# First attention of a four-layer megakernel: sums of two or four window offsets before the output product

## The reference, cut to what matters

```python
        q = _pointwise(Wq, bq, x)
        k = _pointwise(Wk, bk, cond)
        v = _pointwise(Wv, bv, cond)
        k = jnp.pad(k, ((0, 0), (0, 0), (pad_left, pad_right)))
        v = jnp.pad(v, ((0, 0), (0, 0), (pad_left, pad_right)))
...
        dots = jnp.einsum('bhdt,bhdtw->bhtw', qh, k_win) * scale
        attn = jax.nn.softmax(dots, axis=-1)
        out = jnp.einsum('bhtw,bhdtw->bhdt', attn, v_win)
        out = out.reshape(B, C, T)
        return _pointwise(Wo, bo, out)
```

## Time and profile before

| | |
|---|---|
| median of 3 runs | 1675.38 us (1674.85 to 1675.93) |
| the profiled execution's own time | 1682.93 us |
| its span | 1681.6 us |
| mean granted TensorE clock over the span | 0.981 |
| first wide product starts | 119.73 us into the span |
| last addition of `attn0` ends | 238.4 us |
| wide products and what hangs on them | 118.7 us, 7% of the span |

### The profile page before, as it was taken

One profiled execution on the slowest core, in us unless ns is written; L12 is line 12 of the kernel. 1 busy time (PEld: TensorE's weight loads), 2 busy tenths in 40 slices (PEclk: granted clock), 3 DMA queues, 4 the chain that ended last, 5 costly groups with the idle time before them and its releaser, 6 DMA issues.

```text
span 1681.6 us, 22246 instructions
## 1 busy us (share of the span) xinstructions
PE 1602.4 (95%) x9380; PEld 1156.9 (69%) x9380; DVE 1003.3 (60%) x1328; ACT 470.8 (28%) x682; POOL 567.4 (34%) x402
## 2 busy tenths in 40 slices
PE   8979989999989999999999999998999999899998
PEld 2264437888658877788787878877755466568786
DVE  5987765223552665564555646554762379786765
ACT  4140012000422334233432323332101456531010
POOL 3907642221244334131432313231132054462211
PEclk9989979999989999999999999999999999999999
DMA  3000032100200211011010110100210121500000
GB/s 127 1 1 0 1 123 79 50 0 32 100 13 0 85 41 63 20 44 38 26 38 26 63 38 26 38 1 1 104 49 1 26 53 28 193 1 13 13 13 13
DMA packets 18019, 66.55 MB, mean 40 GB/s; under 512 B 1440, under 2 KB 9760, under 8 KB 13312
## 3 DMA queue, kind: packets, MB, share of 16 engines
q1 hardware_dynamic: 17920, 65.12, 11.2%
HBM read 58.82 MB, written 2.10 MB: 36 GB/s over the span
## 4 chain that ended last, share of the span: by engine, by line
PE 80%; DVE 12%; ACT 3%; issue 2%; POOL 2%; DMA 1%; SPq 0%; DVEq 0%; ACTq 0%; POOLq 0%
PE banks L270 47%; PE banks L264 27%; PE banks L399 2%; DVE arena L442 2%; PE banks L1913 1%; DVE arena L1434 1%; DVE grouped_split L1466 1%; PE banks L2186 1%; PE banks L1320 1%; DVE arena L234 1%; DVE arena L1421 1%; DVE window L483 1%; ACT arena L1537 1%; ACT arena L1536 1%; POOL up_lo L859 1%
## 5 line engine op out<-in xcount | busy, mean ns | idle before, releaser
L270 PE MATMUL banks<-grouped_split 128*128 128x512 f32 x1536 | 367.4, 395 | 6.8 <-DVE grouped_split L1466 6.1
L270 PEld LDWEIGHTS banks<-grouped_split 128*128 128x128 f32 x1536 | 284.7, 189 | 70.0 <-DVE grouped_split L1466 9.3
L1603 POOL TENSOR_TENSOR arena<-arena,attn_tables 128x512 f32<-128x512 f32 x80 | 102.1, 1281 | 312.7 <-ACT arena L1537 312.7
L270 PE MATMUL banks<-experts_split 128*128 128x512 f32 (+1 forms) x792 | 181.6, 392 | 1.9 <-DVE experts_split L630 1.9
L270 PEld LDWEIGHTS banks<-experts_split 128*128 128x128 f32 (+1 forms) x792 | 146.5, 185 | 36.4 <-issue 2.5
L1421 DVE TENSOR_TENSOR arena<-banks,attn_tables 128x512 f32<-128x512 f32 x80 | 54.7, 684 | 129.9 <-ACT arena L1537 129.9
L264 PE MATMUL banks<-arena 128*128 128x64 f32 (+2 forms) x698 | 111.9, 313 | 14.7 <-DVE arena L1434 6.8
L264 PEld LDWEIGHTS banks<-arena 128*128 128x128 f32 x698 | 96.5, 196 | 36.3 <-issue 27.7
L660 DVE SCALAR_TENSOR_TENSOR arena<-banks,experts,arena 128x512 f32<-128x512 f32 x64 | 47.6, 750 | 106.8 <-PE banks L270 106.8
L1434 DVE TENSOR_TENSOR arena<-arena 128x512 f32<-128x512 f32 x80 | 70.5, 881 | 54.6 <-POOL arena L1603 54.5
L509 POOL TENSOR_TENSOR window<-window 128x1024 f32<-128x1024 f32 x32 | 75.7, 2368 | 73.9 <-DVE window L483 73.9
(11 more groups left out here) (289 smaller groups left out, 2961.3 us busy)
## 6 DMA issues: line engine op xcount, KB each, us to landing
grouped<-in_attn SPq DMA_DIRECT2D x16, 1024.0 KB, 5.0
experts<-in_expert SPq DMA_DIRECT2D x8, 1024.0 KB, 4.8
linear<-in_ffn SPq DMA_DIRECT2D x1, 4096.0 KB, 13.3
grouped<-in_attn SPq DMA_DIRECT2D x8, 512.0 KB, 3.6
dense<-arena SPq DMA_DIRECT2D x16, 256.0 KB, 4.3
dense<-in_w SPq DMA_DIRECT2D x1, 3584.0 KB, 12.0
dense<-in_attn SPq DMA_DIRECT2D x1, 3072.0 KB, 13.5
dense<-in_w SPq DMA_DIRECT2D x1, 2688.0 KB, 10.2
```

What stands on the lines that cost most here:

```text
L270: s = pe.matmul(dst, lhsT=lhsT[i], rhs=rhs[j], start=(k == 0 and x == 0), stop=(k == n - 1 and x == 2))
L1603: g_.tensor_tensor(rot, rot, SIN[:, h * HALF:(h + 1) * HALF], ALU.mult).then_inc(rot_sin.sem, 1)
```

## The change

It changes five things in `attn0`.

1. **Sums.** The 16 offsets of a pair of tiles are dealt into groups of 4, 2, 2, 4, 2, 2. A group of two has one sum, a group of four has three (0+1, 2+3, and the sum of these). GpSimd does 40 sums in place of 32; TensorE does 24 x 2 output matmuls in place of 32 x 2.
2. **Places.** Wide products have three places in PSUM (`WIDE`) in place of two; the accumulators of the output have one pair of banks in place of two. There are 12 slots in place of 8; four of them lie in the memory of k.
3. **Order.** An output product is due 6 offsets behind the last of its group (group of four, or the first group) or 4 behind it, and its two matmuls stand at two neighbouring offsets.
4. **Low parts.** They are computed by four offsets over all 512 positions instead of by 128 positions over all offsets. The first is computed before the first wide product; the other three follow the products n = 0, 3 and 7 on VectorE. ScalarE's last cut of the high part is written in four pieces.
5. **Fillers.** `stay_busy` issues 13 matmuls in place of 22; the additions of a pair of tiles stand at offset 5, its moments at 7 and 9.

```diff
+    SLOTS, SUM = [K0 + j * 2 * D for j in range(4)] + [DOTS + j * 2 * D for j in range(8)], PROD + 2048
+    sizes = (4, 2, 2, 4, 2, 2)
+    groups = [(p * WIN + sum(sizes[:i]), n) for p in range(4) for i, n in enumerate(sizes)]
+    sums = [(first, pair) for first, size in groups for pair in (((0, 1), (2, 3), (0, 2)) if size == 4 else ((0, 1),))]
...
+    WIDE = (0, 2, 6)
...
-        stay_busy(m, pe, 7, 22)
+        stay_busy(m, pe, 7, 13)
...
-        pe.wait_ge(*low_done(4))
...
+        def to_out(k, x):
+            first, size = groups[k]
+            p, i = k // len(sizes), k % len(sizes)
+            pe.wait_ge(*pair_done(last_sum[first] + 1))
+            if i == 0 and p:
+                pe.wait_ge(*add_done(2 * p))
+            s = mm(pe, bank[:, 4 + x, :], f(W0 + 3 * P, P), f(SLOTS[first % 12] + x * D, D), i, len(sizes))
+            if x:
+                s.then_inc(out_mm.sem, 1)
+
+        due = [first + size - 1 + (6 if size == 4 or first % WIN == 0 else 4) for first, size in groups]
         for n in range(4 * WIN):
             p, w = n // WIN, n % WIN
-            if n >= 2:
-                pe.wait_ge(*av_done(n - 1))
+            if n >= 3:
+                pe.wait_ge(*av_done(n - 2))
+            if n % 4 == 0 and p == 0:
+                pe.wait_ge(*low_done(w // 4 + 1))
             for x, part in enumerate((hi, lo)):
                 for i, t in enumerate(PAIRS[p]):
                     rows = slice(t // 2 * 32, t // 2 * 32 + 32)
-                    s = pe.matmul(bank[:, n % 2 * 2 + i, :], lhsT=seltr[rows, t * P:(t + 1) * P], rhs=part[rows, w, :],
+                    s = pe.matmul(bank[:, WIDE[n % 3] + i, :], lhsT=seltr[rows, t * P:(t + 1) * P], rhs=part[rows, w, :],
                                   start=x == 0, stop=x == 1)
             s.then_inc(wide_mm.sem, 1)
-            if n % 2 and n >= 5:
-                to_out((n - 5) // 2)
-        to_out(30)
-        to_out(31)
+            for k in range(len(groups)):
+                for x in range(2):
+                    if due[k] + x == n:
+                        to_out(k, x)
...
-        divide(0)
-        for c in range(1, 4):
+        for c in range(4):
             divide(c)
-            low(c - 1)
-        low(3)
+        low(0)
...
             v.wait_ge(*wide_mm(n + 1))
-            if n >= SLOTS:
-                v.wait_ge(*out_mm((n - SLOTS) // 2 + 1))
...
+            if n - 12 in summed:
+                v.wait_ge(*pair_done(summed[n - 12] + 1))
+            elif n >= 12:
+                v.wait_ge(*out_mm([first for first, size in groups].index(n - 12) + 1))
...
+            if n in (0, 3, 7):
+                low({0: 1, 3: 2, 7: 3}[n])
+            if n in (3, 5, 7, 9):
+                v.wait_ge(*low_done((n - 1) // 2))
-            if w == 7 and p:
+            if w == 5 and p:
                 add(p - 1)
+            if w in (7, 9) and p:
+                moments(p - 1, (w - 7) // 2)
...
+        for n, (first, (to_step, other_step)) in enumerate(sums):
+            to, other = (f(SLOTS[(first + x) % 12], 2 * D) for x in (to_step, other_step))
+            if (to_step, other_step) == (0, 2):
+                g.wait_ge(*pair_done(n))
+            else:
+                g.wait_ge(*av_done(first + other_step + 1))
+            g.tensor_tensor(to, to, other, ALU.add).then_inc(pair_done.sem, 1)
...
-            act.activation(hi[:, :, cut], dots[:, :, cut], ACT.Copy).then_inc(hi_done.sem, 1)
+            for ws in [slice(0, WIN)] if c < 3 else [slice(4 * j, 4 * j + 4) for j in range(4)]:
+                act.activation(hi[:, ws, cut], dots[:, ws, cut], ACT.Copy).then_inc(hi_done.sem, 1)
```

More of the change, by code:

```diff
@@ L299, in attn0 @@
     ATT = DOTS + WIN * D
-    AV, SLOTS, SUM = DOTS, 8, PROD + 2048
+    SLOTS, SUM = [K0 + j * 2 * D for j in range(4)] + [DOTS + j * 2 * D for j in range(8)], PROD + 2048
+    sizes = (4, 2, 2, 4, 2, 2)
+    groups = [(p * WIN + sum(sizes[:i]), n) for p in range(4) for i, n in enumerate(sizes)]
+    sums = [(first, pair) for first, size in groups for pair in (((0, 1), (2, 3), (0, 2)) if size == 4 else ((0, 1),))]
+    summed = {first + pair[1]: n for n, (first, pair) in enumerate(sums)}
+    last_sum = {first: n for n, (first, pair) in enumerate(sums)}
     seltr = m.buf("selt_split", CT, NT * P, F32R)
@@ L307, in attn0 @@
     sub_done, exp_done, sum_mm, sum_done, att_done, hi_done, low_done = (
-        m.sem(n, 4) for n in ("sub", "exp0", "sum_mm", "sum_done", "att", "att_hi", "att_low"))
+        m.sem(n, k) for n, k in (("sub", 4), ("exp0", 4), ("sum_mm", 4), ("sum_done", 4), ("att", 4), ("att_hi", 7), ("att_low", 4)))
     selt_done, wide_mm, av_done, pair_done, out_mm = (
-        m.sem(n, k) for n, k in (("selt_done", 1), ("wide_mm", 64), ("av_done", 64), ("pair_done", 32), ("out0_mm", 32)))
+        m.sem(n, k) for n, k in (("selt_done", 1), ("wide_mm", 64), ("av_done", 64), ("pair_done", len(sums)), ("out0_mm", len(groups))))
     add_done = m.sem("add0_done", NT)
@@ L398, in tensor @@
                     rows = slice(t // 2 * 32, t // 2 * 32 + 32)
-                    s = pe.matmul(bank[:, n % 2 * 2 + i, :], lhsT=seltr[rows, t * P:(t + 1) * P], rhs=part[rows, w, :],
+                    s = pe.matmul(bank[:, WIDE[n % 3] + i, :], lhsT=seltr[rows, t * P:(t + 1) * P], rhs=part[rows, w, :],
                                   start=x == 0, stop=x == 1)
             s.then_inc(wide_mm.sem, 1)
-            if n % 2 and n >= 5:
-                to_out((n - 5) // 2)
-        to_out(30)
-        to_out(31)
+            for k in range(len(groups)):
+                for x in range(2):
+                    if due[k] + x == n:
+                        to_out(k, x)
+        for k in range(len(groups)):
+            for x in range(2):
+                if due[k] + x >= 4 * WIN:
+                    to_out(k, x)
     def vector(v):
@@ L505, in pool @@
                                 ALU.mult).then_inc(prod_g.sem, 1)
-        for k in range(2 * WIN):
-            at = AV + 2 * k % SLOTS * 2 * D
-            g.wait_ge(*av_done(2 * k + 2))
-            g.tensor_tensor(f(at, 2 * D), f(at, 2 * D), f(at + 2 * D, 2 * D), ALU.add).then_inc(pair_done.sem, 1)
-            if k == 27:
+        for n, (first, (to_step, other_step)) in enumerate(sums):
[5 more added lines that the diff above has]
+            g.tensor_tensor(to, to, other, ALU.add).then_inc(pair_done.sem, 1)
+            if n == len(sums) - 6:
                 m.rsqrt_half(g, 1, 0)
```

31 lines of the change are left out of this document (12 added, 19 removed).

## The result

The changed kernel takes 1694.4 us (median of 4 runs, 1692.0 to 1700.7) against 1675.6 us for the kernel before, run beside it: +18.8 us, ratio 1.0114 with a 95% interval of 1.0090 to 1.0139. Slower, as forecast, but by 18.8 us where the forecast had 8.6, and 0.4 us beyond the range.

What follows compares the result with a forecast made beforehand. TensorE was taken to set the pace. 110.7 us at the upper clock, 3.3 for low parts meeting sums and 18.6 for the clock made 132.6 us, ending 8.6 us later: median 1684 us, range 1666 to 1694.

Steps and rivals of the forecast that it cites:

- The sum: First wide product to last addition: 132.6 us from 114.4 us on, ending at 247.0 in place of 238.4 us.
- The start: Before the products: three low parts moved away, so the first wide product starts at 114.4 us, -5.3 us.
- the low parts: Second and third low parts among the products meet GpSimd's sums: GpSimd loses 4.5 us, net +3.3 us, between 0 and 9.
- Eight offsets without additions: One round of eight offsets at the upper clock takes 12.8 us, against 12.2 before.
- dense part: In each round, six output matmuls with three wide products between them, VectorE following TensorE: 7.4 us at the upper clock.
- its distance to the median, 7.55 us, I keep: Whole kernel: the profiled 1691.5 us less the old profile's 7.55 us distance to its median gives 1684 us.
- The clock term: A dip in each of seven rounds, after five wide products in a row: 2.65 us a round, 18.6 us, bounds 0 and 44.
- Additions: Moving the additions to offset 5 and moments to 7 and 9 costs VectorE the same time, hidden behind output work: nothing.
- Rival A: Clock stays up, or dips stay within the wide products: -10.0 us, 1665.4 us; chance 0.22 together with D.
- B: Gains and losses cancel, about 1.4 us lost a round instead of 2.65: 1675 us; chance 0.13.
- C: Clock hardly ever comes back, 5 us lost a round: +25 us, 1700 us; chance 0.12.
- D: GpSimd's 40 sums set the pace: -20 us, 1655 us alone, otherwise TensorE waits for sums; chance 0.22 together with A.

Runs made afterwards that it cites:

- e3_lows_first: The changed kernel with all four low parts in front of the first wide product and 28 fillers to cover them: 1688.9 us.
- e0_before: The kernel before, unchanged, run and profiled a second time: 1676.3 us.
- e7_spread_fill: The changed kernel with one output matmul to an offset, 17 fillers at the start and one before two of three wide products in each run: 1670.7 us.
- e5_spread: The changed kernel with output matmuls dealt out one to an offset, additions at offset 7, moments at 9 and 11, no added fillers: 1727.3 us.
- e14_joined: The changed kernel, its groups kept, with both matmuls of an output product at one offset: 1685.1 us.
- e4_pairs: The changed kernel with groups of two alone, wide and output matmuls alternating one and one: 1689.5 us.
- e11_pairs_joined: The changed kernel with groups of two alone and both matmuls of an output product at one offset: 1685.1 us.

## Why the prediction was right and where it was wrong

**The direction was right, and the clock as what costs.** The sum gave 132.6 us from the first wide product to the last addition and an end at 247.0 us; the profile shows 132.0 and 245.8. The start came out 0.6 us better than its term. GpSimd lost 4.1 us to the low parts (forecast 4.5), shown by e3_lows_first. Eight offsets without additions take 12.9 us at the upper clock (from 171.4 to 184.3 us; forecast 12.8). Profile against profile, the change costs 9.1 us, forecast 8.6.

**That the sum met the profile so closely is in part luck.** It gave each of the six later rounds of eight offsets a dip, 6 x (12.8 + 2.65) or 92.7 us. They took 91.1: two of them 12.9 us without any dip, the others 14.7 to 19.1, additions included. The 12.9 us are not made of what the forecast made its 12.8 of either, TensorE following VectorE for five offsets and VectorE following TensorE: the chain of those rounds runs through three of GpSimd's sums, for which the forecast had no term outside the first dense part. And the sign that it named for the low parts, one of 3 us or more beside a sum, didn't show: they took 2.28 to 2.42 us, and it was two sums that took 4.4 us each in place of 2.36. Both of those low parts had started 0.2 us before their sum (121.31 and 121.54 us, 128.17 and 128.34); in the earlier trace rows it was GpSimd's operation that had started first, and VectorE's that took longer.

**The step that failed** is the last one: "its distance to the median, 7.55 us, I keep". The profile of before was a run with 65 us at the lower clock against a median of 47; 18 us times 0.391 is 7.0 of the 7.3 us by which it lies over this comparison's median. Of its dips, 27.3 us lay in the very stretch under study, where e0_before has 13.7, so they belong to the kernel's spread and aren't an offset that a changed kernel inherits. The changed kernel's profiled run was the fastest of its four, 2.5 us under their median. 7.3 and 2.5 are the 9.7 us between 9.1 and 18.8. The prediction read three dips of 3.4, 3.4 and 10.2 us as the kernel's habit; e0_before has one of 3.4 us behind the start.

**The clock term** was the right term: in the medians the changed kernel has 50 us more at the lower clock, and 0.391 of that is 19.5 us, all of the 18.8. At no time at the lower clock the two kernels would be level, 1656.7 and 1657.8 us (an extrapolation, over 97 us for the changed kernel; e7_spread_fill against e5_spread, 57 us between two kernels that differ by fillers alone, needs none). So in this order the work that TensorE saves hardly pays at the upper clock either: eight offsets without additions take 12.9 us there, and 12.2 in the kernel before. The term was reckoned as 18.6 us against no dips at all; what I never worked out is the same term for the kernel before. Nor were the dips alike: two long ones, 20.5 and 23.9 us, and three of 3.4 to 6.8 us, not one of 5.7 in each round. The Trainium skill's rule, in "TensorE: Matmul & The Clock Gate", section "Why this matters for your kernels", names long idle gaps as what brings the clock down. In e5_spread it stayed down for 160 us with TensorE busy for 95% of them, so here that rule would have missed the main effect.

**Two terms were mis-sized and passed unseen.** Alternation: I took 0.56 and 0.957 us from runs of eight and four; a wide product between output matmuls takes 0.66 and a single output matmul 1.05, so a dense part at the upper clock takes 3 x 0.66 + 2 x 1.91 + 2 x 1.05 = 7.9 us, not 7.4, 3.5 us over seven. Since the eight offsets came at 12.9 us all the same, the rest of the round was shorter than its term by nearly as much. Additions: I put them at nothing behind the dense part, but they stand in the run of wide products. The first two rounds with them take 15.8 and 14.7 us, dips of 6.8 and 3.4 us included, against 12.9 with neither; what is the additions' and what the clock's was not taken apart. The kernel before has this too (14.0 and 14.2 us against 12.2 in e0_before, at the upper clock), so it hardly moves the difference.

**Rival A** gave 1665 us for a clock that stays up. The level of the change, plus 0.391 for each of the 33 us at the lower clock that lie outside the stretch in its profile, is 1670 us: a gain of some 6 us, not 10. Its 10 us too were reckoned against a stretch with 27.3 us of dips; with e0_before's 13.7 they would be 5 less, so nearly all of the gain that is left is what the kernel before's own dips cost. **B, C**: the time was neither B's 1675 us nor C's 1700. **D**: GpSimd didn't set the pace alone; it was idle for a quarter of the stretch. But it was in the chain for 30% of it, the waits that D spoke of came, 6.5 us of them, and what they cost stays open: e14_joined has 2.8 us of them, but another order too.

Open: what of TensorE's work ends a dip. TensorE was busy for 92% of the 23.9 us dip, and the clock came back while two output matmuls stood in a row; before that, two in a row had not done it.

## What to carry to other kernels

A saving on the engine that sets the pace can be taken back by its clock: here a quarter fewer output matmuls, dealt out so that TensorE did nothing but wide products for five offsets at a time, doubled its time at the lower clock and cost 19 us. The same sums with the output matmuls dealt out evenly and 30 fillers in the thin places gave a gain of 5 us. An engine that is idle for a quarter of a stretch can still be in its chain: look where its results are waited for. Before costing a change from one profile, compare its clock with that of the other runs of the same kernel: dips inside the stretch under study are neither an offset nor a habit. Cost an instruction from a place where it stands between the same neighbours as it will.

## What the runs showed of the hardware that I had not expected

- Single matmuls that alternate between the two kinds (32 rows in pairs of row groups, and 128 rows of float32) pay about 0.2 us at each change: 1.72 us for one and one, 3.04 for two and two (e4_pairs, e11_pairs_joined).
- The lower clock can hold for 160 us under a TensorE busy for 95% of the time, and whether it does depends on fillers that take 0.65 us each: 1727 against 1671 us (e5_spread, e7_spread_fill).
- A sum on GpSimd took 4.4 us in place of 2.36 beside a VectorE operation of 2048 columns with both inputs in SBUF, which itself took 2.4 us: GpSimd was held up and VectorE hardly. VectorE's had started 0.2 us before; where GpSimd's had started first, VectorE's was the one that took longer.
- Runs of one kernel on one chip differ by up to 12 us (the kernel before, 29 runs of 1673.6 to 1686.1), nearly all of it the time at the lower clock.
